# A perceiver block on one Trainium2 core: half of the value-output weight products are made in the attention instead of in the heads

## The reference, cut to what matters

```python
kv_rope = kv_c * cos + rotate_half(kv_c) * sin
q_r    = einsum(einsum(layernorm(x) @ Wq.T, w_kc_q), W_qr)      # per head, width 64
k_r    = einsum('bld,hdr->bhlr', kv_rope, W_kr)
attn   = softmax(einsum('bhsr,bhlr->bhsl', q_r, k_r))
ctx_c  = einsum('bhsl,bld->bhsd', attn, kv_rope)
ctx_lat = einsum('bhsd,hkd->bshk', ctx_c, w_kc_kv)
x = x + ctx_lat.reshape(b, s, H * K) @ Wo.T
```

## Time and profile before

| | us |
|---|---|
| median of 3 runs | 1013.42 |
| lowest, highest run | 1009.63, 1014.2 |
| the profiled execution | 1011.37 |
| its span, first to last instruction | 1009.5 |
| busy: PE, DVE, ACT, POOL | 956.6, 530.1, 413.0, 453.4 |

### The profile page before, as it was taken

One profiled execution on the slowest core, in us unless ns is written; L12 is line 12 of the kernel. 1 busy time (PEld: TensorE's weight loads), 2 busy tenths in 40 slices (PEclk: granted clock), 3 DMA queues, 4 the chain that ended last, 5 costly groups with the idle time before them and its releaser, 6 DMA issues. The chain is left out here.

```text
span 1009.5 us, 15936 instructions
## 1 busy us (share of the span) xinstructions
PE 956.6 (95%) x5497; PEld 807.7 (80%) x5497; DVE 530.1 (53%) x975; ACT 413.0 (41%) x956; POOL 453.4 (45%) x489
## 2 busy tenths in 40 slices
PE   6999977999899989999999999989999999999987
PEld 5777756888778868888888988767779899999977
DVE  4443358777788735454444223338866333333335
ACT  1444458777878724343222233543332122222111
POOL 1798866555667510000000303137607978990041
PEclk9999999999999999999999999999999999999989
DMA  7499813111111105223310025220016656751142
GB/s 248 159 269 266 239 55 95 43 43 38 38 32 41 46 1 188 84 83 101 125 45 21 14 59 156 88 100 2 23 65 210 224 194 204 231 184 50 52 145 96
DMA packets 79003, 109.92 MB, mean 109 GB/s; under 512 B 14224, under 2 KB 46992, under 8 KB 78928
## 3 DMA queue, kind: packets, MB, share of 16 engines
q1 hardware_dynamic: 66288, 82.18, 26.7%
q10 hardware_dynamic: 10080, 18.35, 5.2%
q0 software_dynamic: 2560, 8.39, 2.5%
HBM read 83.13 MB, written 25.77 MB: 108 GB/s over the span
## 5 line engine op out<-in xcount | busy, mean ns | idle before, releaser
L43 PE MATMUL psum<-second_xT_hi,second_w_hi 128*128 128x512 f32 x272 | 106.8, 393 | 4.9 <-PEq L74 2.9
L45 PE MATMUL psum<-second_xT_hi,second_w_lo 128*128 128x512 f32 x272 | 106.0, 390 | 0.0
L44 PE MATMUL psum<-second_xT_lo,second_w_hi 128*128 128x512 f32 x272 | 106.0, 390 | 0.0
L1239 POOL TENSOR_TENSOR all_x<-all_x,mlp_raw 128x512 f32<-128x512 f32 x8 | 10.0, 1288 | 173.1 <-DVE all_x L1741 173.1
L2259 ACT ACTIVATE moe_s<-psum 128x352 f32<-128x352 f32 x39 | 18.1, 465 | 156.1 <-PE psum L45 136.8
L2325 DVE TENSOR_TENSOR moe_hT_lo<-psum,moe_hT_hi 128x384 fp32r<-128x384 f32 x39 | 21.7, 558 | 83.0 <-ACT moe_hT_hi L2265 83.0
L43 PEld LDWEIGHTS psum<-second_xT_hi,second_w_hi 128*128 128x128 f32 x272 | 51.0, 188 | 17.4 <-issue 3.5
L1696 ACT ACTIVATE mlp_s<-psum,mlp_side 128x512 f32<-128x512 f32 x32 | 21.8, 682 | 100.2 <-PE psum L45 100.2
L43 PE MATMUL psum<-moe_w_hi,moe_tT_hi 128*128 x184 | 61.3, 333 | 0.0
L1741 DVE TENSOR_TENSOR all_x<-all_x,psum 128x512 f32<-128x512 f32 x64 | 43.8, 686 | 31.6 <-PE psum L45 31.2
L45 PEld LDWEIGHTS psum<-second_xT_hi,second_w_lo 128*128 128x128 f32 x272 | 51.1, 188 | 10.8
(11 more groups left out here) (344 smaller groups left out, 2868.3 us busy)
## 6 DMA issues: line engine op xcount, KB each, us to landing
kv_all<-all_x ACTq DMA_DIRECT2D x28, 256.0 KB, 4.9
far_raw<-in_eg SPq DMA_DIRECT2D x10, 704.0 KB
far_raw<-in_eu SPq DMA_DIRECT2D x10, 704.0 KB
slot_rows<-mix_W SPq DMA_DIRECT2D x23, 256.0 KB, 5.9
slot_out<-far_rows ACTq DMA_DIRECT2D x23, 256.0 KB, 2.3
far_raw<-in_ed SPq DMA_DIRECT2D x10, 512.0 KB
far_rows<-slot_rows ACTq DMA_DIRECT2D x19, 256.0 KB, 3.3
second_raw<-in_w_feat SPq DMA_DIRECT2D x18, 256.0 KB, 3.5
```

The lines of the kernel that those rows point to most:

```text
L43: e.matmul(out, hi_l, hi_r, start=first, stop=False)
L44: e.matmul(out, hi_l, lo_r, start=False, stop=False)
L45: return e.matmul(out, lo_l, hi_r, start=False, stop=last)
L1239: pool.tensor_tensor(g["x"][:, t, :], g["x"][:, t, :], b2, ALU.add).then_inc(x_plus, 1)
```

## The change

- In the heads only G of heads 0 to 7 is made (`LATE_G = H // 2`). `fold_g(2 * p)` behind the first query product is gone; behind the second stands `fold_g(p + 1)`, for p below 7, and so for `keep_g` and `split_g`. Raw weights are loaded in rounds 0, 2 and 4 only.
- In the last round ScalarE splits the queries of steps 0 and 1 directly after one another.
- The raw weights of heads 8 to 15 go to a tensor of their own name, `late_raw`, which lies at the same addresses as `G_hi` and `G_lo`: the raw weights of a head lie where the two parts of its product go. Five loads bring them (512 KB each), at the start of SyncE's attention program, before its wait for the last rotation.
- In the attention TensorE folds heads 8 to 15 behind the scores of steps 0 to 5: two, two, one, one, one, one (`LATE_AT`). Banks are OB, and CT for the second and fourth. Fold i waits for the low part i - 2 to be done (`late_ok` at least i - 1), from i = 5 on for low part i - 1.
- ScalarE makes the high part one step later, before its exponentials; VectorE makes the low part in that same later step, behind the maxima.
- context(0) also waits for four low parts, and the first output product for all eight.

```diff
@@ heads: sync
-                if p + 1 < NP:
-                    load_g(p + 1)
+                if p % 2 == 0 and p + 2 < LATE_G:
+                    load_g(p // 2 + 1)
@@ heads: tensor
                     queries(p, 0)
-                    fold_g(2 * p)
                 turn_context(BPP * p + 2)
                 queries(p, 1)
-                fold_g(2 * p + 1)
+                if p + 1 < LATE_G:
+                    fold_g(p + 1)
                 turn_context(BPP * p + 3)
@@ heads: scalar (vector: split_g likewise)
                     keep_queries(p, 0)
-                    keep_g(2 * p)
                 context_columns(BPP * p + 2)
...
                     first_queries(0)
-                keep_g(2 * p + 1)
-                if p + 1 == NP:
                     first_queries(1)
+                if p + 1 < LATE_G:
+                    keep_g(p + 1)
@@ attention
+        LATE_AT = ((0, 1), (2, 3), (4,), (5,), (6,), (7,))
+        NLATE = H - LATE_G
+        kckv, woT = (a[:, LATE_G * D:].rearrange("p (u j) -> p u j", j=D) for a in late_raw)
+        kckv = kckv[:, :, 0:P]
+        def late_bank(i):
+            return CT if i in (1, 3) else OB
...
+            sp.dma_start(kckv, d["kckv"][LATE_G:H].rearrange("u p k -> p u k")).then_inc(late_in, 16)
+            for i in range(0, NLATE, 2):
+                sp.dma_start(woT[:, i:i + 2, :], d["woT"][(LATE_G + i) * P:(LATE_G + i + 2) * P, :]
+                             .rearrange("(u k) j -> k u j", u=2)).then_inc(wide_in[i // 2], 16)
...
+            def late_fold(i):
+                if i == 0:
+                    pe.wait_ge(late_in, 16)
+                    pe.wait_ge(heads.g_kept, LATE_G)
+                if i == 1:
+                    pe.wait_ge(heads.kvT_ok, B)
+                    pe.wait_ge(heads.first_lo, 2)
+                pe.wait_ge(wide_in[i // 2], 16)
+                wait(pe, late_ok, i - 1 if i < 5 else i)
+                pe.matmul(psum[:, late_bank(i), :], kckv[:, i, :], woT[:, i, :], start=True, stop=True).then_inc(late_ready, 1)
...
                 wait(pe, c_ok, b)
+                if b == 0:
+                    pe.wait_ge(late_ok, 4)
...
-                        pe.wait_ge(heads.g_kept, H)
+                        pe.wait_ge(late_ok, NLATE)
...
                 if s < B:
                     scores(s)
+                if s < len(LATE_AT):
+                    for i in LATE_AT[s]:
+                        late_fold(i)
                 if 0 <= s - 2 < B:
                     context(s - 2)
...
+            def late_hi(i):
+                act.wait_ge(late_ready, i + 1)
+                act.activation(G_hi[:, late_columns(i)], psum[:, late_bank(i), :], ACT.Copy).then_inc(late_hi_ok, 1)
...
             for s in range(B + 2 + BPT):
+                if 0 <= s - 1 < len(LATE_AT):
+                    for i in LATE_AT[s - 1]:
+                        late_hi(i)
...
+            def late_lo(i):
+                v.wait_ge(late_hi_ok, i + 1)
+                v.tensor_tensor(G_lo[:, late_columns(i)], psum[:, late_bank(i), :], G_hi[:, late_columns(i)].bitcast(F32),
+                                ALU.subtract).then_inc(late_ok, 1)
...
                     maxima(s, 1)
+                if 0 <= s - 1 < len(LATE_AT):
+                    for i in LATE_AT[s - 1]:
+                        late_lo(i)
@@ build
+            with ExitStack() as early:
+                late_raw = [Names(nc, early, "late").sb(k, [P, H * D]) for k in ("kckv", "woT")]
             G_hi, G_lo = a.sb("G_hi", [P, H * D], F32R), a.sb("G_lo", [P, H * D], F32R)
```

More of the change, by code:

```diff
@@ L280 @@
 KEPT = 4
+LATE_G = H // 2
 EARLY = (18, 20, 22, 24, 26, 30, 34)
@@ L718, in vector @@
                     keep_queries(p, 0)
-                    split_g(2 * p)
                 keep_queries(p, 1)
@@ L722, in vector @@
                     first_queries(0)
-                split_g(2 * p + 1)
+                if p + 1 < LATE_G:
+                    split_g(p + 1)
             first_queries(1)
@@ L728, in heads_programs, with attention_programs @@
     return made
-def attention_programs(nc, d, g, q, G_hi, G_lo, rows, cols, xT2_hi, xT2_lo, up, heads):
+def attention_programs(nc, d, g, q, G_hi, G_lo, late_raw, rows, cols, xT2_hi, xT2_lo, up, heads):
     psum, x, ident, tailT = g["psum"], g["x"], g["ident"], g["tailT"]
@@ L770, in attention_programs, with late_columns @@
         DONE = 2
+        late_in, wide_in = S_("late_in"), [S_(f"wide_in{i}") for i in range((H - LATE_G) // 2)]
+        late_ready, late_hi_ok, late_ok = S_("late_ready"), S_("late_hi_ok"), S_("late_ok")
+        LATE_AT = ((0, 1), (2, 3), (4,), (5,), (6,), (7,))
[4 more added lines that the diff above has]
+            return CT if i in (1, 3) else OB
+        def late_columns(i):
+            return slice((LATE_G + i) * D, (LATE_G + i + 1) * D)
         MOST = 2.0 ** 126
@@ L2524, in build @@
                 heads = heads_programs(nc, d, g, q, G_hi, G_lo, rows, cols)
-                attention = attention_programs(nc, d, g, q, G_hi, G_lo, rows, cols, xT2_hi, xT2_lo, up, heads)
+                attention = attention_programs(nc, d, g, q, G_hi, G_lo, late_raw, rows, cols, xT2_hi, xT2_lo, up, heads)
                 phase_opening(nc, heads, attention)
```

## The result

The changed kernel is slower: 1029.28 us median (1024.24 to 1038.19, 4 runs) against 1013.81 us (1009.63 to 1015.68, 4 runs), a ratio of 1.0166 with a 95% interval of 1.0126 to 1.0205. That is +16.8 us (12.8 to 20.8) where +10 was forecast; the time lies inside the range, but outside the forecast's own 1020 to 1026. The medians themselves are 15.5 us apart. The profiled execution took 1024.24 us, span 1022.4. It is the fastest of the four; a possible reason stands at the end. A ratio leaves out executions over 1.5% longer than the fastest of their kernel, which medians and counts of runs keep, so the two can differ.

What follows compares the result with a forecast made beforehand. PE was taken as fullest overall, but an ACT and DVE ring as setting the early attention steps. Terms -1.0 + 1.0 + 2.2 + 7.4 + 0.45 gave +10.0 us, 1023.4 us; range 1016 to 1031, the forecast's own 1020 to 1026.

Steps and rivals of the forecast that it cites:

- the ring: Attention steps 2 to 5: fold's wait delays the context product, 8.07 us a step for 5.59; +2.2 and +7.4 us.
- The heads: Rounds before the attention: removing eight folds gives little back, -1.0 us, 0.5 of it from waits between folds.
- The pinning copy: Heads: DVE's copy of the first query product, behind low parts, holds the second query product; PE idles where the fold was.
- The far end: Heads: if every removed fold counts, they lose 8 x 0.96 = 7.7 us.
- the clock: PE's granted clock in steps 2 to 5: 3.2 us gap put between a case that fell and one that stayed.
- steps 0 and 1: First attention steps: maxima of step 2 at 11.3 us after the first scores, for 10.3 before; +1.0 us.
- Rival (a): Clock falls again and again in steps 2 to 5: +5 us, 1028 (1025 to 1033); chance 0.25.
- Step 6: Attention: first output product waits for the last low part, 2.0 us after the maxima instead of about 1.6; +0.45 us.
- Loads: Late raw weights: five issues from 128 to 130 us, in by 140, before they are needed; no cost.
- rival (b): Late weights arrive late, PE waits once in step 0 or 1: +2 to 5 us, 1027; chance 0.08.
- Rival (c): Attention: the fold's wait is hidden by slack and PE's 1.57 us gap; about 1013 us; chance 0.09.
- Rival (d): Heads bound by PE's sum of work, so removed folds give 7.7 us; 1007 us; chance 0.05.

Runs made afterwards that it cites:

- Fold_last: Changed kernel with each step's late folds moved on PE behind the context product and transposes: ratio 1.0031 to the kernel before, median 1017.28 us.
- same_step: Changed kernel with ScalarE's high part and VectorE's low part of a late fold taken in the fold's own step: ratio 1.0042 to the kernel before, 1017.05 us.
- copy_first: Changed kernel with VectorE's copy of the first query product moved ahead of the low parts in rounds 1 to 6: ratio 1.0126 to the kernel before, 1022.99 us.
- Warm: Changed kernel with identity transposes on PE ahead of the late folds of steps 2 to 5 (12, then 24): ratio 1.0114 to the kernel before, 1022.82 us.
- no_late: Changed kernel without the eight late folds, their parts and waits, raw weights still loaded: ratio 0.9962 to the kernel before, median 1014.39 us.
- spread: Changed kernel with two late folds ahead of the first scores, one each in steps 0, 1, 3 to 6: ratio 1.0009 to the kernel before, 1014.48 us.
- before_copy_first: Kernel before, with VectorE's copy of the first query product ahead of the low parts of A and the key weights: ratio 1.0008 to the kernel before.

## Why the prediction was right or wrong

- **The direction and the mechanism of the ring: right.** The ring of maxima, low part, fold, context product, context parts, low part of the probabilities is there link by link, at 8.03 us where the clock is full for 8.07 forecast. Fold_last and same_step take the link out in two different ways, and both fall back to 5.6 us with all work in place. This is shown.
- **The heads: right in kind, the size too low.** 1.84 us for 1.0: by the second query product of round 6 it is 1.2 us for the 0.5 forecast, the last round gives the rest. The pinning copy is shown by copy_first, with the control in the kernel before. The far end, 7.7 us, is excluded.
- **The step that failed: the clock.** The sum took the four steps at full clock, 32.3 us; they lasted 36.7, 4.4 more. Warm gives 4.6 of it back. And steps 0 and 1, forecast at 11.3 us, took 12.75: PE had waited 1.58 us for the first scores, and the two folds behind them ran slow (mean clock 0.69 from 137 to 140). That this too is the clock, copy_first shows: there PE waited 0.60 us, the clock stayed, and the two steps took 11.29. How were misread stands below the list. Of the Trainium skill, "TensorE: Matmul & The Clock Gate", the section on HAM oscillation describes loops in which a wait in each round brings the clock down every time. The trace agrees in kind, with three of four steps at a mean of 0.82, but not in every round: the fourth kept 1.00.
- **Rival (a) is what happened.** It named this with +5, 1028 (1025 to 1033), and had a chance of 0.25. The sign that the prediction gave for it, a granted clock of 0.5 between 150 and 182 us, is in the profile. So the time lies inside the stated range thanks to this rival, not to the forecast. That the heads gave 0.8 us more than forecast made the miss a little smaller, which is luck.
- **Step 6:** 0.41 us for 0.45. **Loads:** they were in time; the four wide ones were issued between 120.1 and 122.2 us, some 4 us earlier than forecast even when this profile's lead of 4.0 us is taken off, and landed 6.1 to 8.6 us later. The first fold started at 135.8. This also excludes rival (b).
- **Rival (c)** (the wait is hidden): out by the 3.24 us that PE waits at the fold. **Rival (d)** (faster, the heads bound by PE's sum of work): out by the 1.84 us of the heads and by rounds of 13.6 us in no_late.
- With the measured terms the sum is -1.84 + 16.55 + 0.41 = 15.1 us, inside the measured 12.8 to 20.8. The 1.7 us from there to 16.8 are assigned to nothing; only one of the four executions was profiled.

**The reading of the earlier trace rows.** The prediction put the new gap of 3.2 us between a case where the clock fell and one where it stayed. It is longer than any single wait in either. Where the clock stayed, PE had waited 1.57 us. Where it fell, the longest wait was 1.93 us (first line, the kernel before). In the changed kernel it was 3.25 us ahead of step 5's fold (second line), and the clock fell.

```profile
148.25 0.58 PE L43 MATMUL psum<-first_xT_hi 128*128 128x256 f32 x1 [1.93 <-POOL first_xT_hi L840]
...
175.99 1.65 PE L911 MATMUL psum<-late_woT,late_kckv 128*128 128x512 f32 x2 [3.25 <-DVE q_G_lo L1082]
```

The length of one wait does not decide it alone: step 2 of the changed kernel lost the clock after a wait of 2.54 us, step 2 of copy_first kept it after 2.54.

What stays open: which executions lose the clock in the heads' gap and how often. It was seen in the profiles of no_late (two rounds) and spread (one), not in those of the changed kernel, same_step, fold_last or warm, whose rounds are of the same length. Ahead of the first scores the profiles agree better: in the five where PE had waited 1.54 to 1.84 us there (the changed kernel, no_late, same_step, fold_last, warm) the clock fell within 2 us after it; in the three where it had waited 0.60 to 0.65 us (the kernel before, before_copy_first, copy_first) it did not.

## What to carry to other kernels

Before work is moved into another engine's idle time, read what the moved instruction waits for and what stands behind it in its queue: a wait that ends in the middle of a ring pushes everything behind it around the ring, and the same instruction some lines later costs nothing. Removing work from a full engine gains only until the next chain, so look for the instruction that starts just when another engine's result arrives: here a copy behind two low parts held each round of the heads at 13.6 us where 13.1 was possible. And a gap on PE can have a second price beside its length: here 4.6 us in four steps, on top of the 9.5 us of the ring itself.

## What the hardware showed beyond what was expected

The kernel before ran its first product with the normalised rows at half speed in the profiled execution, the changed one at full speed, with the same program up to there. The rows, before and after:

```profile
23.18 0.63 PE L44 MATMUL psum<-first_xT_lo,heads_A_hi 128*128 128x512 f32 x1
```

```profile
21.35 0.40 PE L44 MATMUL psum<-first_xT_lo,heads_A_hi 128*128 128x512 f32 x1
```

The same 128x512 pass takes 0.63 us in the changed kernel's step 3, at a granted clock of 0.50. From the start of the product to the next fold it is 5.28 us before (22.59 to 27.87) and 2.90 after (21.02 to 23.92), 2.4 us; the fold of A ahead of it took 3.51 us and 1.90, another 1.6. Together this makes the 4.0 us by which the changed kernel's profile is ahead at the first query product. It varies between profiles and does not come with the change alone: of the ten profiles of this case two have the first query product at 25.2 to 25.6 us, the changed kernel and warm, and eight at 28.9 to 29.8. The granted clock of these stretches reads 1.00 in both profiles, so at the start of a trace the duration of a known matmul tells more than that column. It would fit that the profiled execution was the changed kernel's fastest, and that a profile's difference of 12.9 us stands beside a median's of 15.5; the other executions were not profiled, so this is not shown.
